# Left-over dst picks of a graph kernel: one-hots on VectorE, broadcast loads by pairs, and pass 2's first rows loaded during pass 1

## What is computed

```python
# layer 0: two graph convolutions with self-loops, norm = dinv[src] * ew * dinv[dst]
h = relu(segment_sum((x @ W1)[src] * norm, dst) + b1)
h = sigmoid(segment_sum((h @ W2)[src] * norm, dst) + b2)
x2 = layernorm(x + h)
# layer 1: attention over the edges
z = x2 @ fc_w.T;  rh = edge_attr @ fc_r_w.T
e = leaky(z[src] @ aw[0] + z[dst] @ aw[1] + rh @ aw[2])
alpha = softmax of e over the edges of one dst
agg = segment_sum(alpha * (z[src] + rh), dst)
out = layernorm(x2 + relu(agg + z @ loop_w))
```

## Time and profile before

| what | value |
|---|---|
| median of 3 runs | 3388.99 us (3383.53 to 3392.19) |
| span of the profiled execution, first to last instruction | 2442.5 us |
| the profiled execution's own time | not listed beside its span; 3388.99 - 2442.5 = 946.5 us lie around the span if it was like the median |
| mean granted clock of TensorE in the span | 0.854 |
| pass 2's gathers | 1502.4 to 2393.3 us |
| stretch between the last sum of pass 1 and the first of pass 2 | about 1493 to 1616 us |

### The profile page before, as it was taken

How to read it: one execution, slowest core, us unless ns; L and a number is a source line. 1 busy time by engine, 2 the same in 40 slices (tenths; PEclk the granted TensorE clock), 3 DMA queues, 4 the chain that set the end, 5 groups by cost and what they waited for, 6 DMA issues and landing times.

```text
span 2442.5 us, 40269 instructions
## 1 busy us (share of the span) xinstructions
PE 1839.8 (75%) x13148; PEld 1626.2 (67%) x13148; DVE 1772.0 (73%) x7010; ACT 1049.6 (43%) x1686; POOL 1770.9 (73%) x1813
## 2 busy tenths in 40 slices
PE   5777668898889687788888783146889788668966
PEld 4656667777778566677777673045778677658866
DVE  7998878888788446676677564178776976586686
ACT  0010012433234135676867666612565268326821
POOL 7777777777775377777777775777777777777771
PEclk9567889999999889899988886567889899879988
DMA  5224222222222423444444433764445555555550
GB/s 142 60 79 134 64 67 74 77 82 78 69 83 64 116 70 100 112 119 126 134 122 118 117 107 92 179 180 134 131 127 150 148 140 132 139 145 134 138 136 20
DMA packets 273634, 270.98 MB, mean 111 GB/s; under 512 B 43718, under 2 KB 218973, under 8 KB 273406
## 3 DMA queue, kind: packets, MB, share of 16 engines
q1 hardware_dynamic: 202366, 142.27, 20.3%
q0 software_dynamic: 57664, 119.62, 19.6%
q10 hardware_dynamic: 13392, 6.46, 0.9%
HBM read 254.63 MB, written 13.96 MB: 110 GB/s over the span
## 4 chain that ended last, share of the span: by engine, by line
POOL 28%; DVE 24%; PE 22%; issue 14%; DMA 7%; ACT 3%; SPq 2%; ACTq 0%; POOLq 0%; DVEq 0%
POOL ring L694 28%; PE ps L829 6%; DVE SR L1535 5%; DVE SR L1572 5%; PE ps L881 5%; DMA ring<-h_d,srcC 2%; PE ps L856 2%; DMA ring<-x_d,srcC 2%; PE ps L869 2%; DMA U<-dlo_d 2%; PE ps L831 2%; DVE U L1612 1%; DVE U L1673 1%; PE ps L843 1%; DVE SR L1645 1%
## 5 line engine op out<-in xcount | busy, mean ns | idle before, releaser
L694 POOL DMA_INDIRECT ring<-x_d,srcC x1132 | 1129.8, 998 | 367.0 <-issue 347.9
L829 PE MATMUL ps<-SR,ring 128*128 128x128 f32 x3604 | 628.9, 308 | 90.8 <-DMA ring<-h_d,srcC 38.1
L694 POOL DMA_INDIRECT ring<-h_d,srcC x526 | 499.7, 950 | 208.1 <-issue 201.7
L829 PEld LDWEIGHTS ps<-SR,ring 128*128 128x128 f32 x3604 | 552.1, 221 | 112.4 <-issue 74.0
L1645 DVE TENSOR_SCALAR SR<-iota_r,cols 128x288 f32<-128x288 f32 x686 | 342.1, 562 | 150.0 <-PE ps L881 150.0
L881 PE MATMUL ps<-SR 128*128 128x288 f32 x1372 | 362.0, 416 | 0.0
L831 PE MATMUL ps<-SR 128*128 128x128 f32 x1564 | 315.0, 296 | 6.0 <-DVE SR L1572 6.0
L881 PEld LDWEIGHTS ps<-SR 128*128 128x128 f32 x1372 | 260.4, 196 | 67.9 <-issue 2.8
L1186 ACT COPY SR<-ps 128x512 f32<-128x512 f32 (+1 forms) x182 | 99.3, 559 | 398.2 <-PE ps L869 398.1
L1572 DVE TENSOR_SCALAR SR<-iota,rankC,ewC 128x128 f32<-128x128 f32 x972 | 264.3, 363 | 1.4 <-DVE U L1776 0.3
L831 PEld LDWEIGHTS ps<-SR 128*128 128x128 f32 x1564 | 258.1, 213 | 6.3 <-issue 6.1
(11 more groups left out here) (286 smaller groups left out, 2578.3 us busy)
## 6 DMA issues: line engine op xcount, KB each, us to landing
SR<-in_edge_attr_dram SPq DMA_DIRECT2D x97, 512.0 KB, 4.3
U<-dlo_d SPq DMA_DIRECT2D x98, 256.0 KB
SR<-low_d SPq DMA_DIRECT2D x84, 256.0 KB
ring<-x_d,srcC POOLq DMA_INDIRECT x1132
ring<-h_d,srcC POOLq DMA_INDIRECT x526
ring<-in_edge_attr_dram SPq DMA_DIRECT2D x12, 512.0 KB
U<-lo_d SPq DMA_DIRECT2D x18, 256.0 KB
ring<-low_d SPq DMA_DIRECT2D x36, 128.0 KB
```

The source lines that it names most:

```text
L694: pool.indirect_dma_start(ring[:, ring_at(p, h if p < 2 else q), k, 0:width], None, (x if p == 0 and h < R0 else table)[:, :], bass.Indire ...
L829: last = nc.tensor.matmul(ps[(p * NA + k) % 2][:, at], ring[:, ring_at(p, h), j, 0:D], S[:, gg % NS, j, :], start=False, stop=stop)
```

## The change

The left-over picks (groups 72 to 97, 13 pairs) are made otherwise. Their one-hots come from DVE, one compare of 128 x 1024 bf16 with the partition index a group, in place of two ACT passes. From pair 37 on dlo is loaded by pairs (2048 values a partition) into four buffers `dloP`, which lie in the memory of rh slots 3 to 6; pair 36 uses the two old buffers. SP issues the first four pair loads, three edge_attr groups and 13 of 17 banks of x2 within pass 1, at h = HS[1] - 2 = 64, after waits for the sets' last sums and look-ups; the remaining pairs, four banks of x2, then dR, then edge_attr groups 3 to 7 follow. DVE dots groups 0, 1 and 2 between the picks. `junk` and `dR` change places in U.

```diff
+REST = picks_at(HS[1] - 1).stop // 2
+NP_DLO = 4
...
+        dloP = Z[:, 3 * GT * W:(3 + NP_DLO) * GT * W].bitcast(BF16).rearrange("p (a g n) -> p a g n", a=NP_DLO, g=2)
...
+            def load_pair(i):
+
+                b = (i - REST - 1) % NP_DLO
+                if i - REST - 1 >= NP_DLO:
+                    sp.wait_ge(s("ohd_made"), 2 * (i - NP_DLO) + 2)
+                sp.dma_start(dloP[:, b].rearrange("p g n -> p (g n)"), dlo_d[2 * i * GT * P:2 * (i + 1) * GT * P].rearrange("(a n) -> a n", a=1).broadcast_to([P, 2 * GT * P])
+                             ).then_inc(rh_loaded[3 + b], 16)
+
+            def load_x2(k):
+                b0, b1_ = home(k)[0], home(k)[-1] + 1
+                sp.wait_ge(*stored(x2_stored, k))
+                sp.dma_start(rows[:, b0:b1_, :], x2_d[b0 * P:b1_ * P, :].rearrange("(b p) d -> p b d", p=P)).then_inc(s("x2_loaded"), 16)
...
             for h in range(HS[1] + 4):
+                if h + 2 == HS[1]:
+                    sp.wait_ge(s("slot_summed"), NB * len(RUNS))
+                    for i in range(REST + 1, REST + 1 + NP_DLO):
+                        load_pair(i)
+                    for d in range(3):
+                        load_rh(d, d)
+                    sp.wait_ge(s("looked"), len(RUNS) * NC)
+                    for k in range(NA - 4):
+                        load_x2(k)
...
-            for q in range(picks_at(HS[1] - 1).stop, G - 2):
-                load_dlo(q + 2)
-            sp.wait_ge(s("looked"), len(RUNS) * NC)
-            for k in range(NA):
...
+            for i in range(REST + 1 + NP_DLO, G // 2):
+                load_pair(i)
+            for k in range(NA - 4, NA):
+                load_x2(k)
...
-            sp.wait_ge(s("set_added"), len(RUNS))
-            for d in range(NR):
-                load_rh(d, d)
             sp.wait_ge(s("picked"), G // 2)
             load_drows(0)
             load_drows(1)
+            for d in range(3, NR):
+                load_rh(d, d)
...
-            for q in range(picks_at(HS[1] - 1).stop, G):
-                begin_pick(q)
...
+            def begin_picks(i):
+
+                for q in (2 * i, 2 * i + 1):
+                    if i == REST:
+                        dve.wait_ge(lo_loaded[q % 2], 16 * (R0 // 2 + q // 2 + 1))
+                    else:
+                        dve.wait_ge(rh_loaded[3 + (i - REST - 1) % NP_DLO], 16 * ((i - REST - 1) // NP_DLO + 1))
+                    dve.wait_ge(s("pick_summed"), q - 1)
+                    low = dloB[:, q % 2, :] if i == REST else dloP[:, (i - REST - 1) % NP_DLO, q % 2, :]
+                    v.tensor_scalar(ohD[:, q % 2, :], low, pidx[:, 0:1], None, ALU.is_equal).then_inc(s("ohd_made"), 1)
...
+            begin_picks(REST)
+            for i in range(REST, G // 2):
+                for k in (NA - 3, NA - 2, NA - 1):
+                    if node_tiles(k)[0] // GT // 2 == i:
+                        node_table(k)
+                if i + 1 < G // 2:
+                    begin_picks(i + 1)
+                if i - REST in (2, 4, 6):
+                    rh_dot((i - REST) // 2 - 1)
                 end_pick(i)
...
-            for q in need(0):
-                rh_dot(q)
+            assert [*need(0)] == [0, 1, 2]
             edge_scores(0)
```

More of the change, by code:

```diff
@@ L320, in build @@
         pre = preX[:, :, :, 0:D]
-        junk = U[:, 3872:3872 + NJ * P].rearrange("p (a d) -> p a d", d=P)
+        junk = U[:, 0:NJ * P].rearrange("p (a d) -> p a d", d=P)
+        dloP = Z[:, 3 * GT * W:(3 + NP_DLO) * GT * W].bitcast(BF16).rearrange("p (a g n) -> p a g n", a=NP_DLO, g=2)
         iota_i = U[:, 0:NARROW].bitcast(I32)
@@ L334, in build @@
         most, far, near = (U[:, 3296 + k * 16:3296 + k * 16 + NSET] for k in range(3))
-        dR = U[:, 0:2 * 386].bitcast(I32).rearrange("p (a n) -> p a n", a=2)
+        dR = U[:, 3872:3872 + 2 * 386].bitcast(I32).rearrange("p (a n) -> p a n", a=2)
         same, pen = U[:, 772:772 + 385], U[:, 1157:1157 + 385]
@@ L440, in rh_turns @@
         def rh_turns(q):
-            return 16 * (q // NR + 1) + 16 * (q == G - 1)
+            pairs = len(range(REST + 1 + (q % NR - 3), G // 2, NP_DLO)) if 3 <= q % NR < 3 + NP_DLO else 0
+            return 16 * (q // NR + 1 + pairs) + 16 * (q == G - 1)
         def closed(p, k):
@@ L573, in _ @@
                         sp.dma_start(x2_d[b0 * P:b1_ * P, :].rearrange("(b p) d -> p b d", p=P), preX[:, k % 2, 0:b1_ - b0, :]).then_inc(x2_stored[k % 2], 16)
-            for q in range(picks_at(HS[1] - 1).stop, G - 2):
-                load_dlo(q + 2)
-            sp.wait_ge(s("looked"), len(RUNS) * NC)
-            for k in range(NA):
-                b0, b1_ = home(k)[0], home(k)[-1] + 1
-                sp.wait_ge(*stored(x2_stored, k))
-                sp.dma_start(rows[:, b0:b1_, :], x2_d[b0 * P:b1_ * P, :].rearrange("(b p) d -> p b d", p=P)).then_inc(s("x2_loaded"), 16)
+            for i in range(REST + 1 + NP_DLO, G // 2):
+                load_pair(i)
+            for k in range(NA - 4, NA):
+                load_x2(k)
             def load_drows(o):
```

## The result

| kernel | median of 4 runs, us | lowest to highest |
|---|---|---|
| before | 3388.22 | 3383.53 to 3392.19 |
| changed | 3348.89 | 3339.44 to 3357.17 |

The ratio is 0.9881 [0.9857, 0.9905]: the change makes the kernel faster by 1.2%, 39 us. Forecast were 3399.6 us and no gain.

A forecast was written before the change was run, and what follows sets the result against it. It took POOL's gapless gather stream in pass 2 as the bound. A start 7.1 us later, a stream 3.5 longer and tail 0 gave +10.6 us on 3389.0, 3399.6 us; range 3380 to 3410.

The forecast's parts named there:

- the value of the picks: Pass 1 to pass 2 seam: group 0 summed some 60 us sooner, worth 0 in the end time.
- that cover: Start of pass 2: POOL's gather stream hides the picks; without it the 60 us would count.
- The assumption that hid it: Around the profiled span: 946.5 us lie outside it if that execution was like the median; left alone.
- the ring does fill in a run without the profiler: Behind group 0 in pass 2: cheaper gathers make POOL stop before the change, not after; 3375 us; chance 0.13.
- The loads that move: SP's queue late in pass 1: 6.31 MB ahead of x2 stores delay the gathers' start, +7 us, bounds 0 and +13.
- the stores get by: SP's queue: x2 stores aren't held up, only DVE's hold on POOL is left, 3392.5 us; chance 0.22.
- One-hots on DVE: Pick stage: 26 one-hots on DVE hold up POOL's gathers, +3.5 us, bounds 0 and 7.8.
- The prediction's estimate from that page: Pick stage: by the skill's exclusion rule one-hots cost gathers 0.46 us a pair, 6.0 us in all.
- The tail: From the last gather to the kernel's end: softmax, sums and norms, change 0, 46 to 50 us expected.
- the signs listed: Changed profile: expected load times, waits, first and last gather, picks' end, group 0's sum and long gathers.
- The forecast of +10.6 us: Whole kernel: gathers start 7.1 us later, stream 3.5 longer, tail 0, on a span of 2442.5 us.

The follow-up runs named there:

- after_timed: The changed kernel, unedited, timed again beside the kernel before on one chip: 3382.82 us, ratio 0.9845 to the kernel before.
- solo picks: Changed kernel, but POOL begins pass 2's gathers only when all 49 pairs are picked: 3345.83 us, ratio 0.9881 to the kernel before.
- shallow in all passes: Changed kernel, first pass-2 gathers paced by picks, x2 loads behind last x2 stores, POOL's lead 6, 6, 8 groups: 3163.95 us, 0.9248 of before.

## Why the prediction was wrong

**The step that failed is the value of the picks: "Value in the end time: 0, because POOL's stream hides it; before, POOL needed this only by 1624.5."** That is what happens on the chip that was profiled: there group 0 was summed 57 us sooner, and the stream took 887.9 us in both kernels. On the chips of the timed runs the seam lasts 214 us from the first gather to the sum of group 0 (2106.4 to 2320.1), the ring is full after 120, and POOL stood 94.2 us. After the change it stood 43.0. The text had the price for this case, "if that cover were gone the 60 us would count": they did, as 51.2. So it was the cover that the prediction had wrong, and the size that it gave for the uncovered work was nearly right.

The gain from rows: ring wait -51.2, wait at hidden2(16) +8.8 (0.56 to 9.36), together -42.4 us. Measured were 39.3 on the chip of the result and 52.2 on another. The two profiles come from different chips, and their full sum has more in it: the first gather is 16.2 us later (2106.4 to 2122.6), the gathers' stretch 67.6 shorter (1176.0 to 1108.4), and with 0.3 us less of tail this makes the 51.8 by which the spans differ. In the stretch are 51.2 at the ring and 19.7 in POOL's later waits for PE (142.8 to 123.1), with small change elsewhere. The 19.7 are no sure part of the change: in `after_timed`, the same kernel, the stretch was 1129.0 with the same ring wait. Nor is it sure that the 8.8 belong in the sum, since on the chip of `after_timed` the first gather was no later for them.

**The assumption that hid it** stood in the sum: "Around the span lie 3389.0 - 2442.5 = 946.5 us if the profiled execution was like the median of the three; I leave that alone." In every run since, the span is the time less 1.7 to 1.9 us. A gap of 946 us was the sign that margins of the profile (here the 1.8 us by which the ring did not fill) didn't hold for the timed runs.

**The rival "the ring does fill in a run without the profiler"** named the right place and sign, and had too small a chance. Its cause, a gather that costs less, is wrong: gathers cost 947 ns there. The ring fills because PE, DVE and ACT get on slowly beside the gathers. Nor is the profiler enough by itself: profiled executions took 2438 us on one chip and 3339 on another. But every timed execution here lists a span and a clock, so none is known to have run without a recording of some kind, and whether that has a part in the slow kind is open.

**The loads that move** were sized right: priced 7.1 us with bounds 0 and 13, the wait at hidden2(16) grew by 10.9 us on the 2440 chip and by 8.8 on the other kind; without loads in front of the stores it is 0.2 to 0.7, and with 4.2 MB of them 4.0. The queue is served in order, and "the stores get by" is out. The first gather came 20.7 us later on the 2440 chip; 10.9 are this wait; the other 9.8 had arisen before any moved load was issued.

**One-hots on DVE** were priced at 3.5 us with bounds 0 and 7.8, and cost nothing in the total: 887.9 us for 686 gathers either way. In the pick stage some gathers are longer (1.15 instead of 0.94 in the row at 1520.99), but the first 20 took 24.5 us from first to last start instead of 19 x 1.244 = 23.6, 0.9 in all. The Trainium skill, "SBUF — State Buffer", section "SBUF: two separate sides", makes the two engines exclude each other for a whole instruction. The prediction's estimate from that page was 6.0 us here. The longer single gathers agree with it, the sum does not: the trace shows 0.9 us there and 0 over the pass.

**The tail** is nearly unchanged, 49.5 to 48.7 us on the 2440 chip and 106.9 to 106.6 on the other kind.

Of the signs listed, on the 2440 chip nearly all came: the wait of 5 to 12 us (11.2), the last pick before 1550 (1544.0), group 0 by 1565 (1562.1), five gathers of more than 1.0 us in the pick stage (5 to 15), POOL without a long wait on PE, the last gather at about 2403 (2406.6). Outside were the first gather, at 1519.6 and not at 1507 to 1514, and the moved loads, issued from 1486.2 on instead of 1479.4, with the queue full until about 1512 instead of 1500 to 1504. The forecast of +10.6 us was right in sign there, at +17 to +20. It was a forecast for a chip that none of the result's timed runs was on.

**What stays open.** That the picks go slowly while POOL gathers, and not while it stands, is shown by solo picks (24 us against 143). What in the gathers does it (their issue by POOL, their descriptors or their traffic), was not tried. Nor is it known what sets the two kinds of chip apart. The rows read like a limit on how fast instructions are completed, with a backlog in front of it: the gaps grow from pick to pick (0.9, 3.2, 4.6, 7.4 us) up to 22, matmuls follow each other by 2.80 us and steps of DVE by 1.4, and the waits last 14 us beyond POOL's last gather. That is argued from the trace; no run tests it.

## What to carry to other kernels

Compare the profiled span with the timed median first; where they differ by more than the few microseconds of a launch, the profile is of another kind of run, and no margin read from it decides anything. Where one engine runs ahead through a ring, ask of every edit behind it what is left undone when the ring is full, and put a price on both answers. A producer that runs far ahead is not free. On the slower kind of chip, cutting the lead in pass 1 from 18 groups to 6 was worth 3%, and holding the first gathers of pass 2 back until the picks were over lost nothing (ratio 0.9881, as for the change itself).

## What the runs showed of the hardware

- The same kernel took 2438 to 2441 us in one set of runs and 3385 to 3435 in six others, with gathers of the same 0.94 us. The difference is in the waits. While POOL issued gathers back to back, PE, DVE and ACT waited for each other's updates from 1.2 to 22 us, once 44.6, and once it had stood for some 14 us, 0.2 to 0.4 us.
- In those stretches a step of DVE that waits for the one before came 1.4 us behind it instead of 0.24, matmuls with no wait between them started 2.80 us apart, and picks of 8 matmuls 22.40 us apart, with one-hots from ACT and from DVE alike.
- The lower granted clock of TensorE there (0.77 against 0.85) goes with a PE that waits: the seam's windows are at 0.50, the 1.2 GHz level, in both kinds (the earlier trace rows and the window of 2123 to 2267), and shallow in all passes has 0.803.
- 20 loads of 6.31 MB ahead of a store in SP's queue held the store's landing up by 9 to 11 us, at 305 GB/s in the window of 2095 to 2115.
